# The read-out of a chunked mLSTM with the PSUM banks of its two head parities exchanged for the second 64 tokens

## The reference, cut to what matters

```
qk = einsum('bhsd,bhtd->bhst', qh, kh) / sqrt(64)
C = qk * D                                   # D = exp(log_D - row maximum), lower triangle
normalizer = maximum(|sum(C)|, exp(-max_log_D))
h = einsum('bhst,bhtd->bhsd', C / (normalizer + 1e-6), vh)
x = x + headwise_layernorm(h) * norm_w
...
gate, y = fp4_linear(ln(x), w_gate), fp4_linear(ln(x), w_up)
x = x + fp4_linear(silu(gate) * y, w_down)
```

## Time and profile before

| | before |
|---|---|
| median of three runs | 1758.29 us |
| span of the profiled execution | 1759.1 us |
| TensorE (matmul) busy | 1684.1 us, 96% |
| VectorE busy | 1634.2 us, 93% |
| ScalarE busy | 1302.3 us, 74% |
| GpSimd busy | 1155.9 us, 66% |
| mean granted TensorE clock | 0.980 |

### The profile page before, as it was taken

How to read it: one execution, slowest core, us unless ns; L and a number is a source line. 1 busy time by engine, 2 the same in 40 slices (tenths; PEclk the granted TensorE clock), 3 DMA queues, 4 the chain that set the end, 5 groups by cost and what they waited for, 6 DMA issues and landing times.

```text
span 1759.1 us, 41401 instructions
## 1 busy us (share of the span) xinstructions
PE 1684.1 (96%) x13633; PEld 901.1 (51%) x13633; DVE 1634.2 (93%) x3451; ACT 1302.3 (74%) x2700; POOL 1155.9 (66%) x1188
## 2 busy tenths in 40 slices
PE   4578999999999999999999999999999999999997
PEld 3444555555555555555555555555555555555553
DVE  8998999999999989999998999999899999999994
ACT  7777777777877777787777777777877777766653
POOL 8876767666666756676676666666666766666652
PEclk9669999999999999999999999999999999999999
DMA  6446666667567656766665765666566665644432
GB/s 212 139 94 141 145 144 144 133 145 159 129 149 143 145 129 151 153 139 145 137 153 128 154 147 138 144 137 160 123 153 142 147 143 139 147 96 112 102 69 61
DMA packets 574454, 240.60 MB, mean 137 GB/s; under 512 B 507520, under 2 KB 514176, under 8 KB 574240
## 3 DMA queue, kind: packets, MB, share of 16 engines
q1 hardware_dynamic: 574240, 237.96, 59.6%
HBM read 140.35 MB, written 31.72 MB: 98 GB/s over the span
## 4 chain that ended last, share of the span: by engine, by line
POOL 45%; issue 44%; POOLq 1%; PE 1%; DMA 0%; DVE 0%; ACT 0%
POOL stage L1140 11%; POOL stage L1085 8%; POOL xw L1118 4%; POOL un L1151 4%; POOL xn L1123 4%; POOL vk L1110 4%; POOL vc L1102 3%; POOL D L1078 3%; POOL rs L1093 2%; POOL rs L1129 2%; POOL sch L1074 0%; POOL nb L1133 0%; PE bank L643 0%; PE bank L644 0%; PE bank L645 0%
## 5 line engine op out<-in xcount | busy, mean ns | idle before, releaser
L515 PE MATMUL bank<-wgTh,xqT 128*128 128x512 f16 (+1 forms) x1536 | 556.8, 363 | 6.3 <-DMA xqT<-xqs 5.2
L515 PE MATMUL bank<-wuTh,xqT 128*128 128x512 f16 (+1 forms) x1536 | 555.8, 362 | 0.0
L1085 POOL TENSOR_TENSOR stage<-stage,hs 128x512 f32<-128x512 f32 (+1 forms) x192 | 215.2, 1121 | 143.2 <-DVE stage L1294 143.2
L515 PE MATMUL bank<-wgTl,xqT 128*128 128x512 f16 (+1 forms) x768 | 278.0, 362 | 0.0
L515 PE MATMUL bank<-wuTl,xqT 128*128 128x512 f16 (+1 forms) x768 | 278.0, 362 | 0.0
L643 PE MATMUL bank<-wdTh,work 128*128 128x512 f16 x704 | 268.9, 382 | 7.2 <-DMA work<-stage 7.2
L644 PE MATMUL bank<-wdTl,work 128*128 128x512 f16 x704 | 268.1, 381 | 0.0
L645 PE MATMUL bank<-wdTh,work 128*128 128x512 f16 x704 | 267.8, 380 | 0.0
L515 PEld LDWEIGHTS bank<-wgTh,xqT 128*128 128x128 f16 x1536 | 150.3, 98 | 168.1 <-issue 11.4
L515 PEld LDWEIGHTS bank<-wuTh,xqT 128*128 128x128 f16 x1536 | 150.5, 98 | 147.7 <-issue 1.1
L1140 POOL TENSOR_TENSOR stage<-stage,hinv 128x512 f32<-128x512 f32 (+1 forms) x192 | 212.8, 1121 | 13.8 <-DVE hinv L1379 13.7
(11 more groups left out here) (208 smaller groups left out, 3663.3 us busy)
## 6 DMA issues: line engine op xcount, KB each, us to landing
mb<-max_dram SPq DMA_DIRECT2D x64, 512.0 KB, 4.3
x<-in_x_dram SPq DMA_DIRECT2D x64, 256.0 KB, 3.3
wb<-warp_dram SPq DMA_DIRECT2D x128, 128.0 KB, 3.1
cn<-in_ctx_dram SPq DMA_DIRECT2D x64, 256.0 KB, 3.1
out_dram<-ob SPq DMA_DIRECT2D x64, 256.0 KB, 2.5
xb<-in_x_dram SPq DMA_DIRECT2D x60, 256.0 KB, 2.9
xh_dram<-xb SPq DMA_DIRECT2D x55, 256.0 KB, 2.4
xzb<-xh_dram SPq DMA_DIRECT2D x220, 64.0 KB, 2.6
```

The lines of the kernel that those rows point to most:

```text
L515: i = e.matmul(o[:, 0:width], x, w[:, c, n0:n0 + width], start=first and k < 2, stop=last and k >= 4)
L1085: e.tensor_tensor(blocks(hx[:, n0:n0 + w]), blocks(hx[:, n0:n0 + w]), per_block(hs2[:, n0 // BLOCK:(n0 + w) // BLOCK]), ALU.mult).then_inc ...
```

## The change

For tokens 64 to 127 the two banks are exchanged. Even heads (array rows 0 to 63) now write tokens 0 to 63 to R2 and tokens 64 to 127 to R0; odd heads the other way about. Both groups of products follow the same rule, so each PSUM element still gathers its own two parts. The order and shape of the products stay. A bank now holds the even heads for one half of the partitions and the odd heads for the other, so the copy out of one bank is split by halves of the partitions, each to its own place in uc. That is four copies of 64 x 260 in place of two of 128 x 260. The semaphore of a bank is raised by the second copy of that bank.

```diff
 for half in HALF:
     for par in range(2):
         r = slice(par * DH, (par + 1) * DH)
-        e.matmul(U[par][half, c, :], xw[r, c, half], St[t.slot][r, c, :], start=(c == 0), stop=False)
+        e.matmul(U[par ^ HALF.index(half)][half, c, :], xw[r, c, half], St[t.slot][r, c, :], start=(c == 0), stop=False)
...
-        i = e.matmul(U[par][half, c, :], D[:, par, c, half], vc[t.parity][:, 2 * c + par, :], start=False, stop=(c == HC - 1))
+        i = e.matmul(U[par ^ HALF.index(half)][half, c, :], D[:, par, c, half], vc[t.parity][:, 2 * c + par, :], start=False, stop=(c == HC - 1))
...
-e.copy(uc[:, :, :].rearrange("p (c r) d -> p r c d", r=2)[:, k], U[k]).then_inc(s_uc[k], 1)
+for n, half in enumerate(HALF):
+    i = e.copy(uc[half, :, :].rearrange("p (c r) d -> p r c d", r=2)[:, k ^ n], U[k][half, :, :])
+i.then_inc(s_uc[k], 1)
```

## The result

The changed kernel takes 1783.14 us, the median of four runs (1782.19 to 1783.95). The kernel before has a median of 1758.36 us over four runs. The ratio is 1.0139, with a 95% interval of 1.0126 to 1.0151: slower by 24.8 us, outside the forecast range of 1754.5 to 1764.5. The profiled execution took 1782.19 us and its trace has a span of 1780.4 us, 21.3 us more than the span before.

What follows compares the result with a forecast made beforehand. TensorE was taken to bound the steady part, VectorE the start. Products 0, steady part 0, end 0 and start +1.1 us on a median of 1758.29 gave 1759.4 us, with an 8-in-10 range of 1754.5 to 1764.5.

Steps and rivals of the forecast that it cites:

- what lies behind the copies: Steady part after ScalarE's copies: VectorE shifts 0.57 us against TensorE without adding up; +0, to +3 us.
- The copies' size: ScalarE's copies out of PSUM: four take 1.23 us against 0.66 for two, +0.57 us a turn, range +0 to +0.85.
- The products: TensorE's two groups of products: the bank exchange costs 0, range -9 to +22.4 us.
- The first rival: TensorE's first group (L608): row halves exclude each other in one bank, +22.4 us plus start, 1781.8 us; chance 7%.
- The first rival's sign in the trace: TensorE's first product group would take 0.98 us to the second group's start, in place of 0.63.
- The tightest hand-over: Gate turns: VectorE ends the gate rows 0.37 us before TensorE loads them; no shift expected there.
- the second rival: Gate turns: the shift reaches TensorE and carries into the start, +3 and +2.3 us, 1763.6 us; chance 9%.
- The start: First 200 us, four tiles, bounded by VectorE: later copies cost +1.1 us, range 0 to +2.3.

Runs made afterwards that it cites:

- copies by halves: Changed kernel with its four copies reordered, both banks for tokens 0 to 63, then both for tokens 64 to 127: 1771.52 us, ratio 1.0081.
- the collision alone: Kernel before, banks and copies unchanged, with one extra 128 x 128 ScalarE copy ahead of the third piece's SiLU in every steady turn: 1759.53 us, ratio 0.9998.
- the second run: Changed kernel with the banks exchanged but copied out in two copies of 128 x 260: 1758.36 us, ratio 1.0001.

## Why the prediction was wrong

**The step that failed** is the one on what lies behind the copies: "It does not add up, since VectorE is busy 0.94 of the steady part". It took the shift as a delay of a stream of fixed length, and asked only whether it used up what TensorE had in hand. Two things were missing.

First, there is a loop that I did not write down. VectorE goes from nr to xn; ScalarE then does xz, a cast, a table load, a SiLU and the copies; and these release the next nr. In the kernel before this took 19.55 us on VectorE and 3.90 on ScalarE, 23.45 us in all, and the 1.41 us up to TensorE's 24.86 is the wait ahead of the copies that I quoted as ScalarE's reserve. In the changed kernel VectorE goes from nr (991.58) to ScalarE's xz (1012.51) in 20.93 us, ScalarE needs 4.67 to the next nr, and the sum is 25.60 us, the distance of TensorE's read-outs at 1013.22 and 1038.82:

```profile
991.58 0.17 DVE L1473 SCALAR_TENSOR_TENSOR nr<-uc,cols 128x8 f32<-128x8 f32 x1
...
1011.80 0.68 DVE L1354 TENSOR_TENSOR xn<-xn,xi 128x512 f32<-128x512 f32 x1
...
1017.18 0.17 DVE L1473 SCALAR_TENSOR_TENSOR nr<-uc,cols 128x8 f32<-128x8 f32 x1
```

The loop grew by 0.77 us on ScalarE (the copies are 0.87 longer, and start 0.1 us before the SiLU's end) and by 1.38 us on VectorE, 2.15 us against 1.41 in hand. The copies alone are not above it: in the run with ht and hs moved they still have 0.24 us in hand in most plain turns.

The waits alone are, in the turns that have them, for VectorE has a limit of its own. These are turns from nr to nr in four traces: the kernel before, the changed one, copies by halves, and the collision alone (columns as in rows 2, so the busy time of VectorE is the third after the length):

```profile
1003.46:1028.33 24.87, 24.87 (x203) 13.10 (x201) 23.87 (x50) 18.82 (x40) 16.73 (x17) 1.00 0.71 144
991.58:1017.18 25.60, 25.48 (x206) 13.38 (x204) 25.02 (x50) 19.92 (x41) 17.09 (x17) 1.00 0.66 143
1011.20:1036.55 25.35, 25.00 (x204) 13.14 (x202) 24.94 (x52) 19.72 (x41) 17.06 (x17) 1.00 0.63 143
978.23:1003.52 25.29, 25.29 (x205) 13.31 (x204) 24.96 (x52) 19.65 (x41) 17.08 (x17) 1.00 0.64 145
```

With the waits VectorE is busy for 24.94 to 25.02 us of a turn, with copies of 1.52, 1.29 and 0.66 us: more than the 24.86 us that TensorE takes. In the last two turns nr starts 0.24 and 0.79 us after the copies' end, so there VectorE's own order sets the turn; in the changed kernel it and the path through the copies end within some 0.02 us of each other. The copies' length does two things: from 1.30 to 1.54 us it adds 0.24 us to such a turn, and it decides whether the next turn has the waits again, and so whether VectorE can catch up. The prediction read VectorE's reserve from the average, 0.94 busy. In this plain turn of before it was busy 23.87 of 24.87 us, 0.96; a gate turn, with 3.55 us idle, lifts the average reserve.

Second, the length of VectorE's instructions is not fixed. The shift turned the order of two starts round, ht and un, that had been 0.01 us apart, and ht and hs then waited for GpSimd. Of the 1.38 us by which VectorE's part of the loop grew, ht and hs are +1.80, h's rounding (L1296) +0.44, xs and the second hs -1.01, and small waits the rest. The trace of before held the warning, in an instruction that I did not look at for this: xs (L1334), 128 x 32, took 227 to 928 ns, 852 in the mean. The Trainium skill states the mechanism: SBUF — State Buffer, Who interferes with whom, says that tensor_scalar can, with suitable operands, take the port pair that VectorE shares with GpSimd, and that whoever starts second is blocked until the first has finished. The traces agree in each of the runs where un is the first to start: ht ends 0.06 to 0.07 us after un, whatever un's length and ht's start.

**The copies' size** was off as well. I took +0.57 us, from the overlap of two copies on the same 128 partitions; it was +0.86 to +0.88, the upper end that I had worked out as "four without overlap" (+0.85). The run by halves shows why: the overlap is lost where the partitions change. With +0.64 us, in that run, there was still a loss of 14 us.

**The products** came out as forecast: 0.63 us, no gain and no loss. The first rival gave 1781.8 us, 1.3 us from the result, for a reason that the second run refutes. A right number is no proof of its mechanism. The first rival's sign in the trace, 0.98 us for the first group, is not there.

**The tightest hand-over**, the gate rows, did turn into a wait (7.6 us over 14 gate turns), as the second rival had it, but as a consequence of the late loop. **The start** was sized +1.1 us. Up to the sixth read-out it is 0.3 us between the profiles of before and after; for the run with ht and hs moved it is 0.7 us, and for the runs that kept the pace it lies between -1.6 and +0.7 us. One profile of each can't tell it.

## What to carry to other kernels

Where one engine is busy all of the time, write down the other loops of a turn too, with their own length: the wait that ends each of them is the reserve for everything in the loop together, not for one edit. The other engines' own busy time in one turn is such a limit as well: read it by turn, not from an average over turns of different kinds. Before a stream is shifted against GpSimd's, look for VectorE instructions whose duration varies in the trace; their length depends on who starts first, and 0.1 us can cost 0.9. And split a copy by columns rather than by partitions: four by columns took 0.78 us, four by halves of the partitions 1.54.

## What the runs showed of the hardware

- On ScalarE, a copy out of PSUM starts 0.26 to 0.28 us after the one ahead of it if both are on the same partitions (or the first on all 128 and the second on 0 to 63), and 0.37 to 0.40 us after it, without overlap, if they go from 0 to 63 to 64 to 127 or back. Copies of 64 x 260 and 128 x 260 both take 0.36 to 0.38 us.
- A tensor_scalar of VectorE on 128 x 88 that takes 0.20 us by itself takes as long as GpSimd's running tensor_tensor needs to end, up to 1.22 us; started 0.01 us ahead of it, it takes 0.20.
- Two row halves of TensorE's array can write one PSUM bank at the same time, on different partitions, at full pace: 32 records in 0.63 us either way.
- The waits can settle into a pattern of every second turn, and then 1.8 us of them in such a turn cost nothing here: 25.29 us with them, 24.11 without, against TensorE's two of 24.86.
